# Linear attention in a two-layer kernel: the keys' exponentials times the normalised rows first, the values' weights afterwards

## What is computed

```
xn = layernorm(x, ln_w, ln_b)
q = xn @ Wq + bq
k = xn @ Wk + bk + (1 - mask) * -1e6
q = softmax(q over the 64 numbers of each head)        # 8 heads
k = softmax(k over the 1024 rows)
v = (xn @ Wv + bv) * mask
att = einsum('bnhd,bnhl->bhdl', k, v)                  # 64x64 per head
y = einsum('bnhd,bhdl->bnhl', q, att)
x1 = x + silu(layernorm(y) * (1 + scale) + shift) @ W_out + b_out
```

## Time and profile before

| | us |
|---|---|
| median of 3 runs | 3043.34 (3040.37 to 3046.28) |
| profiled execution, its own time | 3043.58 |
| its span in the trace | 3041.7 |
| PE busy | 2681.5 (88%) |
| DVE busy | 2371.7 (78%) |
| POOL busy | 1875.8 (62%) |
| ACT busy | 1604.4 (53%) |

### The profile page before, as it was taken

One profiled execution on the slowest core, in us unless ns is written; L12 is line 12 of the kernel. 1 busy time (PEld: TensorE's weight loads), 2 busy tenths in 40 slices (PEclk: granted clock), 3 DMA queues, 4 the chain that ended last, 5 costly groups with the idle time before them and its releaser, 6 DMA issues. The chain is left out here.

```text
span 3041.7 us, 32696 instructions
## 1 busy us (share of the span) xinstructions
PE 2681.5 (88%) x11046; PEld 1526.9 (50%) x11046; DVE 2371.7 (78%) x3071; ACT 1604.4 (53%) x2412; POOL 1875.8 (62%) x822
## 2 busy tenths in 40 slices
PE   7999999999999887988978988888898897897974
PEld 3556466466465444554544455455455455454542
DVE  3455454554454489999999999999999998999993
ACT  1222223223222466775875776677676687587550
POOL 0111111221223097798899799799799799889991
PEclk9999999999999977999999999999999998998976
DMA  6012022212214344465675665575566566566653
GB/s 213 7 55 77 28 104 87 94 56 90 90 56 151 121 101 97 107 127 115 146 163 113 148 155 124 135 161 129 131 158 145 121 150 144 125 143 144 161 130 74
DMA packets 261596, 355.29 MB, mean 117 GB/s; under 512 B 21597, under 2 KB 115937, under 8 KB 261434
## 3 DMA queue, kind: packets, MB, share of 16 engines
q1 hardware_dynamic: 202024, 246.38, 26.3%
q0 software_dynamic: 55680, 105.93, 20.0%
q10 hardware_dynamic: 3730, 0.96, 0.2%
HBM read 215.56 MB, written 71.58 MB: 94 GB/s over the span
## 5 line engine op out<-in xcount | busy, mean ns | idle before, releaser
L2011 POOL TENSOR_TENSOR hs<-slots,b_wide 128x2048 f32<-128x2048 f32 x255 | 1269.5, 5006 | 139.8 <-PE bank L1527 139.7
L2205 DVE TENSOR_TENSOR_SCAN hs<-bank,hs 128x512 f32<-128x512 f32 x1024 | 1217.9, 1207 | 24.4 <-ACT bank L1784 22.2
L1784 ACT ACTIVATE bank<-dt,decay 128x512 f32<-128x512 f32 x1022 | 698.9, 691 | 541.7 <-DVE hs L2205 539.1
L1527 PE MATMUL bank<-ident,hs 128*128 128x128 f32 x4096 | 674.5, 294 | 244.7 <-DVE acc L2223 189.9
L1527 PEld LDWEIGHTS bank<-ident,hs 128*128 128x128 f32 x4096 | 512.5, 150 | 731.8 <-issue 265.4
L2223 DVE SCALAR_TENSOR_TENSOR acc<-bank,c_t,acc 128x512 f32<-128x512 f32 x772 | 560.0, 726 | 50.5 <-PE bank L1527 47.7
L1479 PE MATMUL bank<-h_t,w_in 128*128 128x512 f32 x1024 | 507.7, 604 | 1.0 <-ACT h_t L1702 1.0
L2059 POOL DMA_DIRECT2D acc<-scaled x252 | 288.8, 1146 | 51.9 <-DMA acc<-scaled 29.8
L1579 PE MATMUL bank<-w_y,values 128*128 128x512 f32 x512 | 252.7, 599 | 1.3 <-DVE values L2327 1.3
L1490 PE MATMUL bank<-w_out,h_in 128*128 128x512 f32 x448 | 222.9, 622 | 3.5 <-ACT dt L1751 3.5
L802 PE MATMUL bank<-z_t,w_k 128*128 128x512 f32 x512 | 221.2, 592 | 0.9 <-ACT z_t L898 0.9
(11 more groups left out here) (168 smaller groups left out, 3105.3 us busy)
## 6 DMA issues: line engine op xcount, KB each, us to landing
b_wide<-b_rows SPq DMA_DIRECT2D x256, 256.0 KB, 3.6
acc<-scaled POOLq DMA_DIRECT2D x252, 256.0 KB, 5.4
w_in<-in_L_cond_W_in SPq DMA_DIRECT2D x128, 256.0 KB, 4.4
z<-in_x SPq DMA_DIRECT2D x8, 2048.0 KB, 9.2
res<-in_x SPq DMA_DIRECT2D x8, 2048.0 KB, 9.5
h_tiles<-h_t SPq DMA_DIRECT2D x56, 256.0 KB, 2.8
h_in<-h_tiles SPq DMA_DIRECT2D x56, 256.0 KB, 4.1
x_rows<-w_part POOLq DMA_DIRECT2D x28, 512.0 KB, 6.7
```

Source lines behind the costliest of these rows:

```text
L1527: last = nc.tensor.transpose(bank[:, j * P:(j + 1) * P], hs[:, slot, j, t * P:(t + 1) * P], ident[:, :])
L1784: nc.scalar.activation(decay_banks[N % 3][:, :], dt[:, H % 2, j, :], ACT.Exp, scale=g.decay[:, 4 * (H % 2) + j, s:s + 1]).then_inc(da_read ...
L2011: nc.gpsimd.tensor_tensor(hs[:, U % RING, :, :], slots[:, H % SLOTS, :, :], b_wide[:, U % B_RING, :].unsqueeze(1).to_broadcast([P, 4, CHUNK]),
L2205: nc.vector.tensor_tensor_scan(block, decay_banks[N % 3][:, :], block, 0.0, ALU.mult, ALU.add).then_inc(scanned, 1)
```

## The change

The product is reordered: `k^T (z Wv)` becomes `(k^T z) Wv`. V isn't computed. After Q, `values_of` makes M = z^T times `k_exp` (4 banks of 8 matmuls with 512 columns), ACT copies each bank to `m_t`, and 16 products of 128 columns with `w_v` give `att` before scaling. The bias of V needs the masked sums of the key exponentials, which DVE now makes (`masked_sums`: four products with the mask and four sums of 1024 elements; `att_bias`), and two more additions put it into `att`. z stays in SBUF until M is made, so there are two buffers for rows, `g.z` and `g.values`, and x of batch b+1 is loaded once M of batch b-1 is done. The transposes move: halves of y ahead of the first two products of Q, halves of k ahead of the fourth and fifth, halves of q and of the next z between the products of M. All iterations are written out. The last store of `h_t` moves from layer 0 to the start of layer 1.

The diff, cut to its core:

```diff
-MM_FIRST = {"K": 0, "V": 8, "Q": 16}
-MM = {"y": 0, "K": 8, "V": 16, "Q": 24, "W": 32}
+MM_FIRST = {"K": 0, "Q": 8}
+MM = {"y": 0, "K": 8, "Q": 16, "W": 24}
...
+K_BEFORE_Q = (3, 4)
+Q_EXP_BEFORE = ((), (0,))
...
-        z, x_raw, x_mv, x_var, x_rs, values = g.z, g.x_raw, g.x_mv, g.x_var, g.x_rs, g.values
+        zs, x_raw, x_mv, x_var, x_rs = (g.z, g.values), g.x_raw, g.x_mv, g.x_var, g.x_rs
...
         @block.sync
...
                 if cur:
-
-                    if not (isinstance(b, int) and b == 0):
-                        need(sp, mm_empty, mm_use(b - 1, "K") + NT)
-                    sp.sem_inc(passed, 1)
-                    sp.dma_start(mask_add[:, :], mask_rows[bass.ds(b, 1)].rearrange("o s -> (o s)").partition_broadcast(P)).then_inc(mask_loaded, DMA)
+                    need(sp, k_inv_ready, b)
+                    sp.dma_start(mask_in[:, :], mask_rows[bass.ds(b, 1)].rearrange("o s -> (o s)").partition_broadcast(P)).then_inc(mask_loaded, DMA)
                 if more:
 
-                    need(sp, tr_ready, tr_use(b, "z") + NT)
-                    sp.sem_inc(passed, 1)
-                    sp.dma_start(z[:, :, :], batch(x_rows, b + 1)).then_inc(x_loaded, DMA)
+                    need(sp, kv_ready, KV_USES * (b - 1) + KD)
+                    sp.dma_start(zs[(b + 1) % 2][:, :, :], batch(x_rows, b + 1)).then_inc(x_loaded, DMA)
...
-                    store_h(b - 1, 1)
+                    if cur:
+                        store_h(b - 1, 1)
...
         @block.tensor
...
+            def values_of(b):
+
+                need(pe, tr_empty, tr_use(b, "q"))
+                for d in range(KD):
+                    n = mm_use(b, "Q") + NT + (ROWS_KEPT if b > 0 and rows_kept(b - 1) else 0)
+                    need(pe, mm_empty, n + d - (MM_RING - 1))
+                    for t in range(NT):
+                        last = nc.tensor.matmul(banks[d][:, :], zs[b % 2][:, t, d * P:(d + 1) * P], k_exp[:, t, :], start=(t == 0), stop=(t == NT - 1))
+                    last.then_inc(kv_ready, 1)
+                    yield d
+                need(pe, m_kept, KD * b + KD)
+                for i in range(KD):
+                    for d in range(KD):
+                        last = nc.tensor.matmul(banks[3][:, i * P:(i + 1) * P], m_t[:, d, i * P:(i + 1) * P], g.w_qkv["v"][:, d, i * P:(i + 1) * P],
+                                                start=(d == 0), stop=(d == KD - 1))
+                last.then_inc(kv_ready, 1)
+                yield KD
...
+                n = mm_use(b, "Q")
+                for t in range(NT):
+                    if prev and t < 2:
+                        y_turned(b - 1, t)
+                    if t in K_BEFORE_Q:
+                        k_turned(b, K_BEFORE_Q.index(t))
+                    product((n, t), lambda k: z_t[:, k, t * P:(t + 1) * P], lambda k: g.w_qkv["q"][:, k, :])
...
+                for d in values_of(b):
+                    if d < 2:
+                        q_turned(b, d)
+                    elif more and d == 2:
+                        z_turned(b + 1, 0)
+                    elif more and d == 3:
+                        z_turned(b + 1, 1, range(2))
+                    elif more:
+                        z_turned(b + 1, 1, range(2, KD))
...
         @block.scalar
...
+            def keep_m(b, d):
+                need(act, kv_ready, KV_USES * b + d + 1)
+                nc.scalar.copy(m_t[:, d, :], banks[d][:, :]).then_inc(m_kept, 1)
...
+                for half in range(2):
+                    for t in Q_EXP_BEFORE[half]:
                         need(act, q_shifted, NT * b + t + 1)
                         nc.scalar.activation(qy[:, t, :], qy[:, t, :], ACT.Exp).then_inc(q_exp_ready, 1)
...
+                    for t in range(4 * half, 4 * half + 4):
+                        need(act, tr_ready, n + t + 1)
+                        nc.scalar.mul(k_exp[:, t, :], bank(t)[:, :], mask_cur[:, t:t + 1]).then_inc(tr_empty, 1)
+                for t in range(Q_EXP_BEFORE[1][-1] + 1, NT):
+                    need(act, q_shifted, NT * b + t + 1)
+                    nc.scalar.activation(qy[:, t, :], qy[:, t, :], ACT.Exp).then_inc(q_exp_ready, 1)
+                for half in range(2):
+                    keep_m(b, half)
+                    keep_half(tr_use(b, "q"), half, q_t)
+                keep_m(b, 2)
+                if more:
+                    keep_half(tr_use(b + 1, "z"), 0, z_t)
+                keep_m(b, 3)
+                if more:
+                    keep_half(tr_use(b + 1, "z"), 1, z_t)
...
         @block.vector
...
+            def masked_sums(b):
+
+                need(dve, tr_ready, tr_use(b, "k") + NT)
+                for i in range(KD):
+                    nc.vector.tensor_tensor(k_t[:, i, :], k_t[:, i, :], mask_in[:, :], ALU.mult).then_inc(k_masked, 1)
+                nc.vector.reciprocal(k_inv[:, :], k_sum[:, :]).then_inc(k_inv_ready, 1)
+                for i in range(KD):
+                    need(dve, k_masked, MASK_USES * b + i + 2)
+                    nc.vector.tensor_reduce(k_part[:, i:i + 1], k_t[:, i, :], AX.X, ALU.add).then_inc(k_masked, 1)
+                need(dve, k_masked, MASK_USES * b + 2 * KD + 1)
+                need(dve, k_inv_ready, b + 1)
+                nc.vector.tensor_tensor(k_share[:, :], k_part[:, :], k_inv[:, :], ALU.mult).then_inc(k_masked, 1)
+
+            def att_bias(b):
+                need(dve, k_masked, MASK_USES * b + 2 * KD + 2)
+                for h in range(2):
+                    at = slice(h * HEAD, (h + 1) * HEAD)
+                    nc.vector.tensor_tensor(bias_att[at, :, :], g.v_bias[at, :].rearrange("p (i d) -> p i d", i=KD)[:, :, at],
+                                            k_share[at, :].unsqueeze(2).to_broadcast([HEAD, KD, HEAD]), ALU.mult).then_inc(k_masked, 1)
...
-                if cur:
-                    n = mm_use(b, "V")
-                    for t in range(NT):
-                        need(dve, mm_ready, n + t + 1)
-                        nc.vector.tensor_tensor(values[:, t, :], banks[t % MM_RING][:, :], g.v_bias[:, :], ALU.add).then_inc(mm_empty, 1)
+                for i in range(1, KD):
+                    keep_k(b, i)
...
+                need(dve, k_exp_ready, KD * b + KD)
+                masked_sums(b)
...
+                need(dve, k_masked, MASK_USES * (b + 1))
+                for h in range(2):
+                    at = slice(h * HEAD, (h + 1) * HEAD)
+                    need(dve, att_ready, ATT_USES * b + h + 1)
+                    nc.vector.tensor_tensor(g.att[at, :, at], g.att[at, :, at], bias_att[at, :, :], ALU.add).then_inc(att_ready, 1)
...
@@ -1397,6 +1457,7 @@
                     if m == W_IN_RING:
                         load_gate_bias()
                         load_weights()
+                        store_half(nc, g, BATCH - 1, 1)
```

More of the change, by code:

```diff
@@ L640, in _, with store_half @@
             dve.wait_ge(x0_normed, NT)
+def store_half(nc, g, b, half):
+    tiles = g.h_dram.rearrange("b t p (k c) -> b k p t c", k=KD)
+    for k in range(KD):
+        nc.sync.dma_start(tiles[b, k][:, 4 * half:4 * half + 4, :],
+                          g.h_t[:, k, half * 512:(half + 1) * 512].rearrange("p (t c) -> p t c", c=P)).then_inc(g.h_stored, DMA)
 def layer0(nc, a, g):
@@ L743, in store_h @@
                 need(sp, tr_empty, tr_use(b + 1, "y") + 4 * half + 4)
-                for k in range(KD):
-                    sp.dma_start(h_tiles[b, k][:, 4 * half:4 * half + 4, :],
-                                 h_t[:, k, half * 512:(half + 1) * 512].rearrange("p (t c) -> p t c", c=P)).then_inc(h_stored, DMA)
+                store_half(nc, g, b, half)
             def load_ada(i):
@@ L811, in turn, with half_turned, z_turned, y_turned @@
                 last.then_inc(tr_ready, 1)
+            def half_turned(n, half, rows, groups=range(KD)):
+                for i in groups:
+                    turn(n, 4 * half + i, [rows[:, 4 * half + j, i * P:(i + 1) * P] for j in range(4)])
+            def z_turned(b, half, groups=range(KD)):
+                need(pe, z_ready, NT * (b - 1) + 4 * half + 4)
+                half_turned(tr_use(b, "z"), half, zs[b % 2], groups)
+            def y_turned(b, half):
+                need(pe, y_normed, NT * b + 4 * half + 4)
+                half_turned(tr_use(b + 1, "y"), half, qy)
@@ new lines, in k_turned, with q_turned @@
+            def k_turned(b, half):
+                need(pe, k_exp_ready, KD * b + KD)
+                for t in range(4 * half, 4 * half + 4):
+                    turn(tr_use(b, "k"), t, [k_t[:, i, t * P:(t + 1) * P] for i in range(KD)])
+            def q_turned(b, half):
+                need(pe, q_exp_ready, NT * b + 4 * half + 4)
+                half_turned(tr_use(b, "q"), half, qy)
+            def values_of(b):
[14 more added lines that the diff above has]
+                yield KD
@@ L864, in body @@
                     for t in range(ROWS_KEPT):
[L865 to L885, removed]
```

(12 more changed lines are left out.)

222 lines of the change are left out of this document (94 added, 128 removed).

## The result

The changed kernel takes 3011.67 us (median of 4 runs, 3009.52 to 3017.19) beside 3043.61 (4 runs, 3040.37 to 3046.28): a ratio of 0.9896, 95% interval 0.9884 to 0.9909, so 1.0% faster. The forecast was 3008, the range 2999 to 3022. The profiled execution took 3009.61, its span is 3007.8.

The account below looks back on a forecast made before the run. PE's list was taken to bound layer 0 (busy 114.17 of 115 us), with layer 1 unchanged at 2033. Gains of 4.2, 14.4, 10.4 and 4.2 in the iterations and 2.2 at the border make 35.4: 3008, range 2999 to 3022.

Parts of the forecast that it names:

- the rival of slower M products: M's products 11% slower with z as stationary operand, 3.0 per iteration, 24 in all: 3032 to 3037; chance 0.04.
- K, q and z transposes: Spread in halves on PE, the three sets take 3 x 3.50 without a wait, taking 1.90 away per iteration.
- Y's transposes: Behind K, the second half waits 1.2 for ACT's exponentials, table load and Silu; bounds 0 and 2.5.
- the rival of longer waits on ACT: Table switch holds ACT 1.28 more or releases come late; seven iterations lose 9.0: 3017; chance 0.12.
- The last copy of M: Ahead of `att`, PE waits for ACT's copy to `m_t`: 0.1 per iteration, 1.0 in iteration 7.
- Scaling and bias: Ahead of y's products, PE waits 1.2 for DVE's work on `att` (0 to 2); 2.06 in iteration 7.
- DVE's cover: DVE's new sums end 22 to 25 after Q, needed 37.2 after Q: twelve us to spare.
- The step that failed: DVE's norm of y, moved behind K's first two banks, priced at nothing: DVE idle 54 of 115 us.
- The rule for the ring: The ring holds PE up only if a bank waits for three further products, 10.3.
- The border: Between layer 0 and layer 1, four stores fewer: SP ends 2.45 earlier, ACT's last Silu limits the gain to 2.2.
- The rival that it gives some back: Layer 1's clock changes between two levels; another start may cost 5 to 15: 3013 to 3023; chance 0.12.
- The slower rival: PE's clock falls to 1.2 GHz behind M; decides from 4.5 us per iteration; half of K gives 3118; chance 0.03.

Follow-up runs that it names:

- experiment 2: Changed kernel with the transposes of k and of q together again after Q, and ACT's order as before: 3029.88 us, ratio 0.9950.
- experiment 3: Changed kernel without the two additions that put the bias of the values into `att`: 3008.61 us, ratio 0.9883.
- experiment 6: Changed kernel with DVE's products with the mask and sums of the key exponentials made twice: 3023.04 us in one execution.
- experiment 7: Changed kernel with DVE's products with the mask and sums of the key exponentials made three times: 3045.28 us in one execution.
- Experiment 1: Changed kernel with POOL's eight additions of the output bias held back until DVE has normalised y: 3009.55 us, ratio 0.9889.
- experiment 4: Changed kernel with the second half of y's transposes ahead of Q's third product instead of the second: 3007.06 us, ratio 0.9880.
- experiment 5: Changed kernel with POOL's additions behind the norm of y and the second half of y's transposes ahead of Q's third product: 2999.77 us, ratio 0.9853.
- experiment 8: Changed kernel with the last four stores of h_t back in layer 0: 3019.74 us in one execution.

## Why the prediction was right, and where it was off

**The product.** 27.47 for V and 7.14 for `att` against 27.47 for M and 3.64 for the new `att` (720.89 to 724.53): as forecast, and so the rival of slower M products falls.

**K, q and z transposes** without a wait: right, 1.75 a half, and experiment 2 gives back 1.91 of the 1.90 forecast.

**Y's transposes:** 1.2 forecast, 1.19 measured (the half would have started at 656.82 and ended 1.75 later, at 658.57; Q goes on at 659.76). In the changed kernel the table load runs from 655.14 to 656.42 and Silu starts at 656.44, straight from the last exponential. So the 1.28 stands where ACT is busy before it too, and neither the rival of longer waits on ACT nor the drain of the Trainium skill ("ScalarE: Activation LUTs", section "What ACT_TABLE_LOAD costs") shows: its 9.7 would have to be in these seven iterations, and these are off by 5.0 in another place.

**The last copy of M** 0 where 0.1 was forecast, and 0.84 in iteration 7 (M's two last banks start at 925.30 and take 13.74, `att` starts at 939.88). The forecast had 1.0 there, though its own T+0.85 gives 0.85. **Scaling and bias:** 1.21 (1.2), and experiment 3 shows the cause.

**DVE's cover:** 12 us to spare was forecast; DVE stood idle 16 ahead of `att`. The error lies on the safe side: the twelve came from the upper bound of 25 us after Q, with the products at their dearer price. DVE was through 21.4 after Q (687.30 to 708.66), as the four products took 4.62 together, the four sums 4.57 and the small ones 1.1; the 37.2 after Q at which it is needed came out as forecast (687.30 to 724.53). Experiments 6 and 7 put the cover at 16.4.

**The step that failed** is the sentence that prices the norm of y at its new place at nothing: "DVE is idle for 54 of the 115 us of the stretch, and the ring holds PE up only if a bank waits for three further products, 10.3". The rule for the ring was right. What I didn't ask was what else runs at the new place: POOL's eight additions start as soon as the variance is done, and the moved norm now starts with them. It takes 10.53 and not 3.73, DVE comes to K's third bank at 643.88 and K's seventh product has to wait for it. K takes 28.19 from 623.45 to 651.64, where 27.47 were forecast: 0.72 in seven iterations, 5.0 of the 5.4 by which the gain of iterations 1 to 7 fell short (23.6 against 29.0). The other 0.4 is small terms and rounding: y takes 7.22 (616.23 to 623.45) and `att` 3.64, 0.07 more each than forecast, and the last copy 0.1 less. Experiment 1 takes the cause away and finds 5.1. A mean idle share of DVE could not tell this.

**The border:** 2.2 forecast, 2.55 measured; the second layer starts 1.43 behind ACT's last Silu, not the 1.74 that I had taken from SP's last issue.

**What was luck.** The span of the profiled execution got 33.9 shorter, near the 35.4 of the forecast, but 3.2 of that lie at the start, where I take none for the change's; without them it is 30.7, and the missing 5 are the step above. That the median stayed inside the range needed no luck: 5 us were within its width.

**Layer 1** kept its length in the profiled execution. The rival that it gives some back is not supported; but its length differs by 5 us between executions, as much as that rival claimed, so that a single pair of traces says little, and the median of the changed kernel, 3.7 above the forecast, has room for both.

**The slower rival**, PE's clock behind M, showed in small and cost little. No product with `att` behind a wait of about 1 ran below full clock in any of the ten traces. Behind longer waits some did. In iteration 8 PE waits 1.9 behind 3.84 of small products: in experiments 1, 2 and 4 the product that follows ran with a granted clock of 0.81 in its stretch and took 9.01 instead of 7.38.

```profile
941.50:950.50 9.00, 9.00 (x64) 8.82 (x64) 5.02 (x9) 0.00 (x0) 1.04 (x1) 0.81 0.79 281
```

It is the row of experiment 1 (same columns as above); part of that stretch was at 1.2 GHz. In the changed kernel and in experiments 5 and 8 the same product behind the same wait kept 1.00, so the wait alone doesn't decide it. Experiments 6 and 7 make the waits longer: behind 4.71 the clock was 0.67 over 9 us of the product and it took 10.20; behind the wait of 3.09, which experiment 7 has five times, it was 0.81 once, 1.00 three times and 0.67 once. The 10 us that follow each of these stretches of 9 us were at 1.00 again. So a fall cost 1.6 to 2.8 us each time, less than the 4.5 per iteration that the rival needs.

## What to carry to other kernels

Where PE's list is the bound, walk it row by row: the removed and added products, and the time at which each bank's reader is done, gave PE's terms in an iteration to within 0.2, save for one wait. When a step is moved, ask of its new place not only whether its engine is idle but what DVE and POOL do there at the same time: beside POOL's additions the norm took nearly three times as long, while evictions from PSUM and maxima kept their time. Put the halves of a set of transposes so far apart that their reader has finished the first; here a table load and the exponentials ahead of it belonged to that time, and one product more between the halves took the wait of 1.2 away.

## What the runs showed of the hardware

DVE and POOL get in each other's way in two forms here. DVE's norm (one SBUF operand of 128x512, result to SBUF, 0.54 alone) goes on beside POOL's additions, but slowly: eight of each in 10.53 and 10.93, where DVE alone needs 3.73 and POOL alone 9.85. DVE pays nearly all of it. And in iteration 7 of the changed kernel a DVE product of 128x4 elements that usually takes 0.16 stood for the whole of POOL's run:

```profile
918.47 9.83 POOL L977 TENSOR_TENSOR res<-res,out_bias 128x512 f32<-128x512 f32 x8
919.68 8.64 DVE L1025 TENSOR_TENSOR k_share<-k_part,k_inv 128x4 f32<-128x4 f32 x1
```

It ended at 928.32, with POOL's last addition at 928.30; both its inputs are in SBUF. In experiment 6 the same happens to a product of `k_t` with the mask, two SBUF inputs too: it takes 9.90 instead of 1.21 beside POOL's run of 9.84. In iteration 7 this cost nothing in the changed kernel, where DVE still waits 6.35 ahead of `att`. The Trainium skill ("SBUF — State Buffer", section "SBUF: two separate sides") says that DVE and GpSimd share a pair of ports that one of them holds for a whole instruction, in DVE's case for fast modes and for two SBUF inputs against a GpSimd instruction that reads SBUF. The rows agree that such pairs hold each other up; that the norm runs in a fast mode, no row shows. They differ in the price: the norm and the additions one instruction at a time would take 3.73 + 9.85, 13.6, and not 10.9 or a little more, and the small product was not let in between two of POOL's instructions.
